# First attention with transposed values and two-part fp16 query weights, on one Trainium2 core

## What is computed

```python
q = (inputs_q @ Wq).reshape(b, sq, H, HD) * (1.0 / np.sqrt(HD))
k = (inputs_kv @ Wk).reshape(b, skv, H, HD)
v = (inputs_kv @ Wv).reshape(b, skv, H, HD)
attn = softmax(einsum('bqhd,bkhd->bhqk', q, k), axis=-1)
ctx = einsum('bhqk,bkhd->bqhd', attn, v).reshape(b, sq, H * HD)
return ctx @ Wo
...
x = x + _L0_xattn_ref(_layernorm(x, axis=-1), ctx_2048, Wq, Wk, Wv, Wo)
```

## Time and profile before

| | |
|---|---|
| median of three runs | 747.97 us (747.45 to 749.23) |
| profiled execution | 750.32 us, its span 749.0 us |
| TensorE (PE) busy | 670.9 us (90%) |
| VectorE (DVE) busy | 575.8 us (77%) |
| ScalarE (ACT) busy | 371.3 us (50%) |
| GpSimd (POOL) busy | 198.6 us (27%) |
| first score, first matmul behind the first attention | 22.07 us, 497.57 us |

### The profile page before, as it was taken

The page is one execution under the profiler, slowest core; times in us unless marked ns, Lnnn a source line. Parts: engine busy times, 40 slices in busy tenths (PEclk is TensorE's granted clock), DMA queues, the critical chain, the costliest instruction groups (busy, mean ns, idle before and its releaser), DMA issues. The chain is left out here.

```text
span 749.0 us, 13021 instructions
## 1 busy us (share of the span) xinstructions
PE 670.9 (90%) x4894; PEld 426.0 (57%) x4894; DVE 575.8 (77%) x1069; ACT 371.3 (50%) x584; POOL 198.6 (27%) x315
## 2 busy tenths in 40 slices
PE   4899999999999999799899999979998988879743
PEld 3456676667666767476566667744553444334431
DVE  3698876977776787677687776749989999999555
ACT  4553334333433443253334336318868998778711
POOL 3285333343334301240000000016324332223100
PEclk9999999999999999899999999989999999999855
DMA  8456965555555578566366475637977999888900
GB/s 285 122 136 145 205 135 126 129 122 118 124 130 122 119 152 232 115 177 167 84 143 182 115 142 131 151 139 136 187 144 142 189 198 177 141 131 158 171 1 7
DMA packets 330639, 107.29 MB, mean 143 GB/s; under 512 B 297032, under 2 KB 328016, under 8 KB 330320
## 3 DMA queue, kind: packets, MB, share of 16 engines
q1 hardware_dynamic: 330576, 106.45, 66.6%
...
HBM read 32.23 MB, written 0.26 MB: 43 GB/s over the span
## 5 line engine op out<-in xcount | busy, mean ns | idle before, releaser
L804 PE MATMUL psum<-c_nat,eT 128*128 128x256 f16 x1536 | 190.7, 275 | 0.0
L1487 ACT ACTIVATE cT<-psum,bias,q_scale 128x1024 f16<-128x1024 f32 x128 | 153.5, 1203 | 39.7 <-PE psum L1412 33.7
L778 PE MATMUL psum<-cT,qk 128*128 128x512 f16 x768 | 171.0, 379 | 1.2 <-ACT cT L715 1.1
L804 PEld LDWEIGHTS psum<-c_nat,eT 128*128 128x128 f16 x1536 | 152.0, 99 | 26.5 <-issue 0.3
L1412 PE MATMUL psum<-kT,v_space 128*128 128x512 f16 x512 | 144.5, 391 | 20.1 <-DVE tops L1518 15.9
L1518 DVE TENSOR_REDUCE tops<-psum 128x1 f32<-128x512 f32 x256 | 158.1, 679 | 2.4 <-PE psum L1412 2.2
L778 PEld LDWEIGHTS psum<-cT,qk 128*128 128x128 f16 x768 | 74.9, 98 | 86.1 <-ACT cT L715 1.3
L927 DVE TENSOR_REDUCE neg_max<-psum 128x1 f32<-128x2048 f32 x32 | 73.3, 2290 | 33.3 <-PE psum L778 33.1
L1412 PEld LDWEIGHTS psum<-kT,v_space 128*128 128x128 f16 x512 | 45.6, 99 | 91.5 <-DVE tops L1518 61.9
L915 DVE TENSOR_TENSOR e_lo<-e_all,e_hi 128x2048 f16<-128x2048 f32 x32 | 77.5, 2422 | 0.0
L890 ACT ACTIVATE e_all<-psum,neg_max 128x2048 f32<-128x2048 f32 x32 | 63.1, 1973 | 11.3 <-DVE neg_max L929 11.3
...
## 6 DMA issues: line engine op xcount, KB each, us to landing
...
```

The costliest lines, as they stand in the source:

```text
L778: ins = pe.matmul(s_ps[:, n * 512:(n + 1) * 512], c.qk[:, u % 2, q_part, k, :], m.cT[:, b, c_part, 4 * n:4 * n + 4, k, :], start=(k, q_par ...
L804: ins = pe.matmul(u_ps, c.eT[:, v % 2, e_part, j, :], m.c_nat[:, v // H0, c_part, j, :], start=(j, e_part, c_part) == (0, 0, 0), stop=(j, ...
L1487: act.activation(x.y[:, u % 2, q * CHUNK:(q + 1) * CHUNK], m.bank(3 + 2 * (q % 2), 2), ACT.Exp, bias=x.bias[:, u:u + 1], scale=m.q_scale[: ...
```

## The change

1. **PV gives u transposed.** `attend` takes the context tile as stationary operand, in two halves of 128 columns, and the transposed exps as moving one: 96 matmuls of 128 columns (L855) for 48 of 256. The result is already uT. The ScalarE multiplication into `u_sb`, the two transposes and the copy after them go; one ScalarE copy from PSUM (L947) stands in their place. The division by the sum moves to the residual on VectorE, which becomes a `scalar_tensor_tensor` (L992); `inv_sum` gets two columns.
2. **Query and fold in fp16.** The head's Wq and Wk land in one buffer of 128 x 512 and are split: ScalarE scales them twice (L677 to fp32, L680 to fp16), GpSimd subtracts (L687). Query (L658) and fold (L668) become six fp16 matmuls each. The transposed latents are split in the setup, and the query into its parts by ScalarE (L695) and VectorE (`dve_query`, L700, new).
3. **Order.** The splits of unit u + 3 stand at the head of iteration u, on GpSimd before the late remainder and the key tiles. GpSimd's side work is woven in by slots instead of coming after the loop. SyncE loads the query weights of unit u + 4 behind the transposes of the exps. The transposes of `xm` move from slot (19, 2) to (19, 3).

The core of the diff:

```diff
 def sp_load_query(sp, c, s, t, u):
-    h, sem = u % H0, s[f"wqk_in{u % 2}"]
-    sp.dma_start(c.wq_h[:, u % 2, :, :], ...
-    sp.dma_start(c.wk_h[:, u % 2, :], t["wkT"][h * HD0:(h + 1) * HD0, :]).then_inc(sem, 16)
+    h = u % H0
+    if u > 0:
+        sp.wait_ge(s["wqk_up"], 2 * u)
+    sp.dma_start(c.wqk_land[:, 0:D].rearrange("p (k n) -> p k n", k=KD), ...
+    sp.dma_start(c.wqk_land[:, D:2 * D], t["wkT"][h * HD0:(h + 1) * HD0, :]).then_inc(s["wqk_in"], 16)
...
-        if u + 3 < UNITS:
-            sp.wait_ge(s["qk_mm"], u + 2)
-            sp_load_query(sp, c, s, t, u + 3)
...
             sp.dma_start_transpose(c.eT[:, v % 2, 1], c.e_lo[:, :]).then_inc(s[f"lo_turned{v % 2}"], 16)
+        if u + 4 < UNITS:
+            sp_load_query(sp, c, s, t, u + 4)
...
-    for u in range(H0):
+    pool_split_query(pool, c, s, 2)
+    for u in range(UNITS - 3):
+        side.upto(4 * u)
+        pool_split_query(pool, c, s, u + 3)
         if u in (1, 2):
...
+        if u >= H0:
+            side.upto(4 * u + 3)
+            continue
...
     for k in range(KD):
-        ins = pe.matmul(ps[:, 0:P], c.wq_h[:, at, k, :], m.xnT[:, k, b * P:(b + 1) * P], start=k == 0,
-                        stop=k == KD - 1)
+        for w_part, x_part in TERMS:
+            ins = pe.matmul(ps[:, 0:P], weights_qk(c, u, w_part, k), c.xnT[:, x_part, k, b * P:(b + 1) * P],
+                            start=(k, w_part, x_part) == (0, 0, 0), stop=(k, w_part, x_part) == (KD - 1, 1, 0))
...
+def act_split_query(act, c, s, u):
+    act.wait_ge(s["wqk_in"], 32 * (u + 1))
+    if u > 0:
+        act.wait_ge(s["wqk_lo"], u)
+    act.mul(c.wqk_up[:, :], c.wqk_land[:, :], K_UP).then_inc(s["wqk_up"], 1)
+    if u > 1:
+        act.wait_ge(s["qk_mm"], u - 1)
+    act.mul(c.wqk[:, u % 2, 0, :], c.wqk_land[:, :], K_UP).then_inc(s["wqk_up"], 1)
...
+def pool_split_query(pool, c, s, u):
+    pool.wait_ge(s["wqk_up"], 2 * (u + 1))
+    if u > 1:
+        pool.wait_ge(s["qk_mm"], u - 1)
+    pool.tensor_tensor(c.wqk[:, u % 2, 1, :], c.wqk_up[:, :], c.wqk[:, u % 2, 0, :], ALU.subtract).then_inc(
+        s["wqk_lo"], 1)
...
+def dve_query(dve, m, c, s, u):
+    dve.wait_ge(s["q_hi"], u + 1)
+    dve.scalar_tensor_tensor(c.qT[:, 1, :], m.bank(4)[:, 0:P], Q_SCALE, c.qT[:, 0, :], ALU.mult,
+                             ALU.subtract).then_inc(s["q_lo"], 1)
...
+    act_split_query(act, c, s, 0)
+    act.wait_ge(s["xnT_mm"], 1)
+    act.copy(flat(c.xnT[:, 0]), m.bank(0)).then_inc(s["xnT_hi"], 1)
     split(0)
-    act.wait_ge(s["xnT_mm"], 1)
-    act.copy(flat(m.xnT), m.bank(0)).then_inc(s["xnT_out"], 1)
+    act_query(act, m, c, s, 0)
     split(1)
-    act_query(act, m, c, s, 0)
+    act_split_query(act, c, s, 1)
     act_fold_key(act, m, c, s, 0)
...
-        for j in range(4 * q, 4 * q + 4):
+        k = q // 2
+        for j in range(8 * (q % 2), 8 * (q % 2) + 8):
             for e_part, c_part in TERMS:
-                ins = pe.matmul(u_ps, c.eT[:, v % 2, e_part, j, :], m.c_nat[:, v // H0, c_part, j, :],
-                                start=(j, e_part, c_part) == (0, 0, 0), stop=(j, e_part) == (KTB - 1, 1))
+                ins = pe.matmul(u_ps[:, k * P:(k + 1) * P], m.c_nat[:, v // H0, c_part, j, k * P:(k + 1) * P],
+                                c.eT[:, v % 2, e_part, j, :], start=(j, e_part, c_part) == (0, 0, 0),
+                                stop=(j, e_part) == (KTB - 1, 1))
...
             act.wait_ge(s["pv"], v + 1)
-            act.wait_ge(s["inv_sum"], v + 1)
             if v > 0:
-                act.wait_ge(s["uT"], v)
-            act.mul(c.u_sb[:, :], u_ps, c.inv_sum[:, :]).then_inc(s["u_out"], 1)
+                act.wait_ge(s["oT"], v)
+            act.copy(flat(c.uT_sb), u_ps).then_inc(s["uT_out"], 1)
...
+        if u + 2 < UNITS:
+            dve_query(dve, m, c, s, u + 2)
         if u < H0:
             dve_key_tile(dve, m, d, s, 2 * u)
```

More of the change, by code:

```diff
@@ L116 @@
 NORM_STEPS = 4
[L119 removed]
+MIX_AT = dict(norm=(18, 2), again=(18, 3), scaled=(19, 0), plus=(19, 1), xT=(19, 3), qkv0=(20, 0), qkv1=(20, 2),
               turn=(20, 3), squares=(21, 0), product=(21, 1), unit=(21, 2), a=(22, 0), yT=(22, 2), out=(23, 0))
@@ L630, in pool_cross, with weights_qk @@
             pool.tensor_tensor(lo, full, hi, ALU.subtract).then_inc(s["k_cut"], 1)
+    side.rest()
+def weights_qk(c, u, part, k):
+    return c.wqk[:, u % 2, part, k * P:(k + 1) * P]
 def pe_query(pe, m, c, s, u):
-    b, at = u // H0, u % 2
+    b = u // H0
     ps = m.bank(4)
-    pe.wait_ge(s[f"wqk_in{at}"], 32 * (u // 2 + 1))
+    pe.wait_ge(s["wqk_lo"], u + 1)
     if u > 0:
@@ L753, in dve_setup @@
     split(3)
+    dve_query(dve, m, c, s, 1)
     turned(2)
```

85 lines of the change are left out of this document (42 added, 43 removed).

## The result

The changed kernel takes 758.33 us (median of 4 runs, 755.76 to 759.0) against 747.71 (744.2 to 749.23) for the kernel before: ratio 1.0142, 95% interval 1.01 to 1.0185. It is slower by some 10 us; the prediction said 747.2, range 741.5 to 751.5. The profiled execution took 755.76 us, the lowest of the four, with a span of 754.5.

A forecast was written before the change was run, and what follows sets the result against it. TensorE was taken to bound most first-attention units, a VectorE, GpSimd and SyncE chain units 0 to 2, 17, 19, 23 and 26. Terms summed to -0.8 us off the median 747.97: 747.2 us, range 741.5 to 751.5.

The forecast's parts named there:

- rival C: PV matmuls: weight loads show beside the 128 columns, a pair takes 78 ns, +68 us, 815 us; chance 0.05.
- units 17, 19, 23 and 26 together within 3 us of +3.7: First attention: the prediction is wrong if these four units together change by more than 3 us from +3.7.
- rival A: First attention: the new waits are hidden, mx_land stays in VectorE's slack; 738 to 743 us; chance 0.18.
- The steady unit: Units 3 to 15, bound by TensorE: -0.31 us each, -4.0 us in all, called the firm part.
- The setup: Before score(0): ScalarE stops for the second query load, then does both scalings; 0 to 2.6 us, taken as +1.4.
- L1012 moves by 0.9 us in every second unit: Even iterations from 16: two query loads on SyncE delay mx_land, for which VectorE waits; hidden where TensorE binds.
- Unit 26: First attention, unit 26: 0.9 us of later mx_land less the share of two units, +0.6 us.
- Unit 23: First attention, unit 23: 0.9 + 0.35 + 0.4 + 0.15 us, +1.8; the clock also falls after the wait.
- P: Follow-up theory: GpSimd's split slows VectorE's own operations; the prediction took 0.4 to 0.5 us in units 17 and 23.
- Rival B: Chain of units 17, 19, 23 and 26 decides, each paying 1.3 us more; 749.5 to 754 us; chance 0.19.
- L: Follow-up theory: SyncE's query loads stand before mx_land, and VectorE carries that delay between slices; 1.2 us every second unit.
- Q: Follow-up theory: `dve_query`, 0.28 us on VectorE in every unit ahead of key tile and side steps, costs the time.

The follow-up runs named there:

- b_xt: Kernel before with only the transposes of xm moved from slot (19, 2) to (19, 3): 746.04 us, ratio 0.994; run again, 744.54 us, ratio 0.9951.
- b_loads_mid: Kernel before with only SyncE's query loads of unit u + 3 moved behind the eT transposes: 756.08 us, ratio 1.0074.
- b_loads_odd: Kernel before with the query loads behind the eT transposes only in odd iterations from 17 on: 748.82 us, ratio 0.9996.
- a_loads_last: Changed kernel with SyncE's query loads moved to the end of the iteration, behind mx_land: 750.48 us, ratio to the kernel before 1.0016.
- a_last_short: Changed kernel with query loads behind mx_land and GpSimd's split cut to 32 of 512 columns from unit 2 on (time probe): 748.17 us, one execution.

## Why the prediction was wrong

**Right.** TensorE: 56 ns per PV matmul, 0.34 us for query and fold, so that rival C, the visible weight load, is out (the 81 ns of the Trainium skill, "TensorE: Matmul & The Clock Gate", section "Back-to-back issue gap", did not come about: the blocks of the steady units go at 56 ns). Units 0 to 2 (+1.7 for +1.9) and the end (-1.5 for -1.9) came out. The places of the loss were the ones named, 17, 23 and 26, and in 26 by mx_land. By its own sign, units 17, 19, 23 and 26 together within 3 us of +3.7, the prediction is wrong: they came to +11.4. Another of its signs misled: the wait before the diagonals stayed at 0.7 us, and yet rival A did not hold, since unit 17's new waits stand ahead of it.

**Mis-sized.** The steady unit: -0.21 for -0.31, for the two fp32 products behind short matmuls; 13 units make this 1.2 us. The setup: 0 for +1.4. ScalarE did stop 1.3 us for the second landing, but the stop was made good before score(0); and with one profile each this term can't be read to a microsecond, as kernels with one and the same setup (before, b_xt twice, b_loads_mid, b_loads_odd) started score(0) at 20.5 to 22.9 us. Over the seven traces with each setup it started at 21.8 us on average with the old one and at 22.6 with the new, so the term is nearer +0.8. The two query loads take SyncE 1.2 us and not 0.9. The slot (19, 3) was priced at 1.4 us; unit 19 of b_xt is 2.6 us shorter, 1.6 of it the wait.

**The step that failed** is "L1012 moves by 0.9 us in every second unit. Where TensorE binds, it is hidden", and with it the +0.6 and +1.8 of units 26 and 23. I priced each slice as if the one before had been on time, the loads as if nothing else moved the slice, and unit 26 at full clock. For the loads alone the 0.9 us is right in iteration 22 (b_loads_mid). What the runs show in place of the rest:

- *Unit 26, +5.3 us for +0.6.* Its wait grew by 4.1 us; with the loads behind mx_land (a_loads_last) 3.2 of them are gone. Here a delay is carried. In the changed kernel the slice of iteration 24 is issued 1.05 us later than in a_loads_last and takes 4.85 us to land for 3.58, the wait in unit 26 is 3.2 us longer, and the remainder of the exps in iteration 26 starts 4.1 us behind its score for 1.6. How long that landing takes differs between executions (3.5 to 4.9 us), so a part of this is chance. To the wait comes the clock, which I had at nothing here: TensorE was busy 17.3 us at clock 0.85 for 16.1 at 1.00 (with a little less work), and 18.7 at 0.85 in b_loads_mid.
- *Unit 23, +4.8 us for +1.8.* Its wait grew from 3.4 to 7.8 us. Moving the loads takes 1.4 us off (6.4 in a_loads_last), and shortening GpSimd's split as well takes 2.2 more (4.2 in a_last_short). The late remainder of iteration 22 is not the loads' delay come round: it starts 3.57 us behind score(22) in the changed kernel and in a_loads_last alike, 1.89 in a_last_short, and 1.58 before and in b_loads_mid. P is the largest part shown in this unit, half of the longer wait.
- *Unit 21, +1.1 us for -0.3.* It is one of the units where the delay was to be hidden. Moving the loads takes 0.75 us off, and in b_loads_mid a wait of 1.1 us for uT appears there.

For VectorE's 17.8 us before mx_land I had written that what delays that load delays the chain, but I priced it once and by itself. The steps from one slice to the next (landing, VectorE's first half, the remainder of the exps, the transposes of mx_tmp, the next load) share VectorE and SyncE with all else that the change made later. Rival B had the places (but unit 19 got 0.9 us shorter). Its price, 5 us over four units and 749.5 to 754 us, was too low too, and its reason (ScalarE holds back SyncE's load) did not come about: in iteration 22 the loads are issued as soon as the transposes ahead of them are (344.84 + 1.62, and 346.51), and in b_loads_mid they wait for nothing new.

**P** was the term sized too low in unit 23. I took 0.4 to 0.5 us from rows 9 against the 1.0 of rows 7. L976 in the earlier trace rows ran 41.53 to 43.28 us and GpSimd's operation ended at 43.25; L1037 in the earlier trace rows began 302.31, GpSimd's L1124 ended at 302.86, and 0.55 + 0.96 = 1.51 is 0.14 over its 1.37. So it stood for the rest of GpSimd's operation and then took its own time, and both rows say nearly the full price. In the changed kernel the late remainder starts later, and so the same small operation stands longer:

```profile
40.44 4.08 POOL L624 TENSOR_TENSOR c_nat<-cT,c_nat 128x2048 f16<-128x2048 f32 x1
...
41.88 2.67 DVE L1023 TENSOR_SCALAR k_amax<-k_amax 128x16 f32<-128x16 f32 x1
```

It ends at 44.55, the remainder at 44.52. This operation did not share, it stood until GpSimd's had ended. Not every one does: the three of VectorE just ahead of it (L1014, L1018, L1021), beside the same operation of GpSimd, took their usual 0.41 to 0.42 us. "SBUF — State Buffer" in the Trainium skill (shared port pair) says that of two that need the shared pair the later one blocks for the whole instruction; the trace agrees, and I was wrong to say that rows 9 disagree.

**The clock** was a term in units 19 and 23 alone; it is one in unit 26 too: in the changed kernel the granted clock is 0.82, 0.78 and 0.85 in units 19, 23 and 26, where in the kernel before it was 0.83, 0.91 and 1.00.

**Open.** Unit 17's +2.2 us: it is 17.1 us in a_loads_last and 16.2 to 16.4 with the split shortened or moved, so some 1.9 us of it stay without L, P and most of Q. What the 9.9 us of waits of the fold cost by themselves: before, the fold waited for ScalarE's copy of the query alone, now it is behind VectorE's maximum. In a_loads_last it still waits 7.8 us though the time is back at before, so part of these waits only take the place of later ones. It was not tried to put `dve_query` ahead of the maximum. Why the clock falls in one execution and not in another behind the same wait is open too. Unit 19 of b_xt took 17.7 us in one execution and 16.6 in the other, at a granted clock of 0.86 and 0.94; single units can't be read closer than that.
